# Preactivated deformable convolution: three bands of hats ahead, window turns between the pairs, hat rows at a pitch of 8,640 bytes

## The reference

```python
x = x + _L0_conv_ref(_gn(x), Wa, ba, Wb, bb, Wg, bg, Wo, bo)   # a, b, gate, product, output
x = x + _L1_conv_ref(_gn(x), w_off, b_off, w_def)              # deformable 3x3 convolution
```

```python
x = relu(x)
offset = conv3x3(x, w_off) + b_off                 # 18 channels: dy, dx for each of 9 taps
py = base_y + off[:, :, 0]; px = base_x + off[:, :, 1]
samp = bilinear_gather(x, py, px)                  # zero outside the image
out = einsum('bckhw,ock->bohw', samp, w_def)
```

## Time and profile before

| | |
|---|---|
| median of three executions | 1771.32 us |
| the profiled execution | 1764.54 us |
| its span, first to last instruction | 1762.7 us |
| mean granted TensorE clock | 0.976 of full speed |
| TensorE (PE) busy | 1562.9 us, 89% |
| VectorE (DVE) busy | 1103.9 us, 63% |
| ScalarE (ACT) busy | 974.2 us, 55% |
| GpSimd (POOL) busy | 939.1 us, 53% |
| moved by DMA | 337.09 MB, mean 191 GB/s |

### The profile page before, as it was taken

The page is one execution under the profiler, slowest core; times in us unless marked ns, Lnnn a source line. Parts: engine busy times, 40 slices in busy tenths (PEclk is TensorE's granted clock), DMA queues, the critical chain, the costliest instruction groups (busy, mean ns, idle before and its releaser), DMA issues.

```text
span 1762.7 us, 28712 instructions
## 1 busy us (share of the span) xinstructions
PE 1562.9 (89%) x10451; PEld 1150.9 (65%) x10452; DVE 1103.9 (63%) x1908; ACT 974.2 (55%) x1474; POOL 939.1 (53%) x734
## 2 busy tenths in 40 slices
PE   5999999538889999999999989899999899999998
PEld 3787777416666666666666656666666666666665
DVE  6888888625666666555565655656666565565653
ACT  3555555335556655565655655555655566655552
POOL 2555556326555665565565555555565555556552
PEclk9999999759999999999999999999999999999999
DMA  4343343235656666666666666666666666666652
GB/s 141 101 122 114 112 123 106 97 136 209 205 202 208 223 224 217 218 226 224 216 223 219 222 212 209 218 210 226 220 239 209 227 218 218 219 213 220 207 208 89
DMA packets 146137, 337.09 MB, mean 191 GB/s; under 512 B 10697, under 2 KB 77796, under 8 KB 146020
## 3 DMA queue, kind: packets, MB, share of 16 engines
q1 hardware_dynamic: 131620, 309.58, 51.6%
q10 hardware_dynamic: 14400, 25.96, 4.2%
HBM read 273.54 MB, written 61.95 MB: 190 GB/s over the span
## 4 chain that ended last, share of the span: by engine, by line
DMA 46%; POOL 16%; PE 15%; issue 13%; DVE 5%; SPq 3%; ACT 2%; POOLq 0%; ACTq 0%; DVEq 0%
DMA hx_all<-hat_x 41%; POOL weights L1550 10%; PE bank L745 5%; PE pair L717 4%; POOL x_bo L1504 4%; SPq L532 3%; DMA hat_x<-hats 3%; PE pair L790 2%; DVE hats L1280 1%; ACT dist L948 1%; DMA raw<-x_pad 1%; POOL rstd L1478 1%; PE bank L763 1%; POOL xT_lo L1491 1%; PE pair L728 1%
## 5 line engine op out<-in xcount | busy, mean ns | idle before, releaser
L1550 POOL TENSOR_TENSOR weights<-hy_all,hx_all 120x512 f32<-120x512 f32 x576 | 761.7, 1350 | 636.4 <-DMA hx_all<-hat_x 630.1
L745 PE MATMUL bank<-weights,zT 120*128 120x216 f32 (+1 forms) x2816 | 610.5, 347 | 29.2 <-POOL weights L1550 25.2
L745 PEld LDWEIGHTS bank<-weights,zT 120*128 120x128 f32 x2816 | 508.4, 192 | 109.5 <-POOL weights L1550 44.2
L1293 DVE SCALAR_TENSOR_TENSOR samples_lo<-bank,samples_hi 128x432 f16<-128x432 f32 (+1 forms) x704 | 401.8, 590 | 260.5 <-ACT samples_hi L963 253.1
L963 ACT ACTIVATE samples_hi<-bank 128x432 f16<-128x432 f32 (+1 forms) x704 | 364.5, 519 | 296.6 <-PE bank L745 284.3
L717 PE MATMUL pair<-samples_hi,w_hi 128*128 128x512 f16 x576 | 220.2, 382 | 0.9 <-DVE y L1328 0.9
L921 ACT ACTIVATE z<-raw,norm_band 128x690 f32<-128x690 f32 (+2 forms) x128 | 204.9, 1603 | 26.1 <-DMA raw<-x_pad 24.1
L717 PE MATMUL pair<-samples_lo,w_hi 128*128 128x512 f16 x576 | 219.1, 380 | 0.0
L717 PE MATMUL pair<-samples_hi,w_lo 128*128 128x512 f16 x576 | 219.0, 380 | 0.0
L763 PE MATMUL bank<-ident,z 128*120 128x128 f32 x640 | 106.8, 281 | 80.6 <-DVE zT L1314 80.6
L973 ACT COPY zT<-pair 120x512 f32<-120x512 f32 x192 | 112.1, 584 | 75.2 <-DVE hats L1280 43.4
(11 more groups left out here) (144 smaller groups left out, 2079.7 us busy)
## 6 DMA issues: line engine op xcount, KB each, us to landing
hy_all<-hat_y SPq DMA_DIRECT2D x192, 600.0 KB
hx_all<-hat_x SPq DMA_DIRECT2D x192, 600.0 KB
raw<-x_pad SPq DMA_DIRECT2D x68, 276.0 KB, 15.6
x_pad<-hy_all SPq DMA_DIRECT2D x64, 276.0 KB, 3.7
weights<-in_x SPq DMA_DIRECT2D x64, 256.0 KB, 2.9
out<-y SPq DMA_DIRECT2D x64, 256.0 KB, 15.6
hat_x<-hats ACTq DMA_DIRECT2D x64, 216.0 KB
hat_y<-hats ACTq DMA_DIRECT2D x64, 180.0 KB
```

Source lines behind the costliest of these rows:

```text
L745: mm = nc.tensor.matmul(sampled_pair(b)[:, :, at:at + BR * cols], zT[0:WPIX, u, w, :], weights[0:WPIX, u, :, w * WC * BR:(w * WC + cols) * ...
L1293: nc.vector.scalar_tensor_tensor(out=samples_lo[:, u, :, c0:c1], in0=sampled_pair(b)[:, :, 0:c1 - c0], scalar=PIXEL_SCALE, in1=samples_hi[ ...
L1550: nc.gpsimd.tensor_tensor(weights[0:WPIX, u, tap, :], hy_all[0:WPIX, k, :], hx_all[0:WPIX, k, :], ALU.mult).then_inc(weights_ready, 1)
```

## The change

Four things change.

1. The hats are made and stored three bands ahead and not two (`O`, `Q`, `H` at 3), and their place in DRAM has three slots and three semaphores (`AHEAD`). `z` stays at three bands ahead, and moves from behind the middle of the iteration to its start, in front of the offsets.
2. The windows are turned two bands ahead and not one (`T` at 2). The six groups stand apart between the pairs, each behind the pairs of the current band that still read the windows it overwrites (`pairs_until`).
3. `split_offsets`, `make_hats` and the farthest distance get places of their own in the order (`P`, `G`, `R`), as has the cast of `z` (`h`). The prologues go; the loop starts three iterations earlier with the steps that have a band.
4. In DRAM a hat row of 6,144 bytes starts every 8,640 bytes (`PITCH`) and not every 6,144.

Size and number of all transfers and of all instructions stay the same.

```diff
@@ -28,6 +28,7 @@
 PADC = (WINDOWS - 1) * WC + SRC_C
 BLOCKS = -(-PADR // BR)
 RING = 9
+AHEAD = 3
 BW = BR * WW
 PAIRS = WINDOWS // 2
 TGROUPS = -(-WINDOWS // 4)
@@ -54,6 +55,7 @@
 SUM_ROWS = CONST_AT + 3
 TROWS = 3
 CHUNK = TROWS * BW
+PITCH = 2 * 1024 + 112
 IN_OFF = 16 * 3
 IN_SELECT, SELECT_STEPS = 16 * 9, 8
 BAND_STEPS, ROW_STEPS = 12, 2 + 4 * TAPS
@@ -105,8 +107,8 @@
         x1_pad = nc.dram_tensor("x1_pad", [IMGS, CH, BLOCKS * BR, PADC], F32, kind="Internal").ap()
-        hat_rows = [nc.dram_tensor("hat_y", [2, TROWS, SRC_R, CHUNK], F32, kind="Internal").ap(),
-                    nc.dram_tensor("hat_x", [2, TROWS, SRC_C, CHUNK], F32, kind="Internal").ap()]
+        hat_rows = [nc.dram_tensor("hat_y", [AHEAD, TROWS * SRC_R, PITCH], F32, kind="Internal").ap(),
+                    nc.dram_tensor("hat_x", [AHEAD, TROWS * SRC_C, PITCH], F32, kind="Internal").ap()]
         pairs = [ctx.enter_context(nc.psum_tensor(f"pair{i}", [P, 2, 512], F32)) for i in range(2)]
@@ -287,7 +289,7 @@
         located = sem("located")
         dist_ready = sem("dist_ready")
         reached = sem("reached")
-        hat_out = [sem(f"hat_out{s}") for s in range(2)]
+        hat_out = [sem(f"hat_out{s}") for s in range(AHEAD)]
         hat_in = [sem(f"hat_in{g}") for g in range(TROWS)]
         hats_ready = sem("hats_ready")
         hats_cleared = sem("hats_cleared")
@@ -372,6 +374,10 @@
             na = (TGROUPS + 1) // 2
             return n * na + a, n * (TGROUPS - na) + v
+        def pairs_until(n, g):
+            return PAIRS * n + min(2 * g + 2, PAIRS)
         def pair_before(n, p):
             return PAIRS * n + p - 3 if p > 2 else PAIRS * (n - 1) + (9, 10, 8)[p]
@@ -385,12 +391,12 @@
         ORDER = [(step[0], int(step[1:])) for step in (
-            "k0 O0 s0 s1 s2 Q0 k1 T0 k2 s3 H0 T1 T2 k3 s4 T3 s5 T4 k4 T5 c0 s6 c1 z0 k5 s7 "
-            "c2 c3 z1 k6 s8 c4 c5 k7 s9 c6 k8 s10 c7 c8").split()]
-        def landed(n, u, step):
-            return step * (n // 2 + 1)
+            "z0 s0 c0 s1 k0 T0 z1 s2 c1 k1 s3 T1 h0 k2 c2 s4 s5 O0 T2 k3 c3 P0 s6 k4 c4 s7 T3 Q0 "
+            "c5 k5 G0 s8 c6 k6 H0 s9 R0 T4 k7 c7 s10 T5 k8 c8").split()]
+        def hats_landed(n):
+            return hat_out[n % AHEAD], 32 * (n // AHEAD + 1)
         def first_block(n):
@@ -405,21 +411,15 @@
             return raw_in[block % RING], 16 * (block // RING + 1)
-        def bands(eng, stages, prologue):
-            prologue()
-            def band(n, u):
+        def bands(eng, stages):
+            ahead = {"c": -1, "s": 0, "k": 1, "T": 2, "z": 3, "h": 3, "O": 3, "P": 3, "Q": 3,
+                     "G": 3, "H": 3, "R": 3}
+            for n in range(-AHEAD, BANDS + 1):
                 for kind, j in ORDER:
-                    ahead = {"c": -1, "s": 0, "k": 1, "T": 1, "O": 2, "Q": 2, "H": 2, "z": 3}[kind]
-                    if not 0 <= n + ahead < BANDS:
-                        continue
-                    if kind in stages:
-                        stages[kind](n + ahead, (u + ahead) % 2, j)
-            for n in range(BANDS + 1):
-                band(n, n % 2)
+                    m = n + ahead[kind]
+                    if kind in stages and 0 <= m < BANDS:
+                        stages[kind](m, m % 2, j)
         block = ctx.enter_context(nc.Block())
@@ -520,14 +520,17 @@
                 sp.dma_start(out_v[bass.ds(n // BPI, 1), :, bass.ds(n % BPI * BW, BW)]
                              .rearrange("b c q -> (b c) q"), y[:, s, :]).then_inc(y_out[s], 16)
-            def spread_hats(n, s):
-                sp.wait_ge(hat_out[s], landed(n, s, 32))
+            def spread_hats(n):
+                sp.wait_ge(*hats_landed(n))
                 for g in range(TROWS):
                     wait(sp, weights_ready, TAPS * (n - 1) + TROWS * (g + 1))
-                    rows = [hat_rows[0][s, g].rearrange("(o r) c -> o r c", o=1),
-                            hat_rows[1][s, g, g:g + NEAR_C].rearrange("(r o) c -> r o c", o=1)]
+                    y_at, x_at = g * SRC_R, g * SRC_C + g
+                    rows = [hat_rows[0][n % AHEAD, y_at:y_at + SRC_R, 0:CHUNK]
+                            .rearrange("(o r) c -> o r c", o=1),
+                            hat_rows[1][n % AHEAD, x_at:x_at + NEAR_C, 0:CHUNK]
+                            .rearrange("(r o) c -> r o c", o=1)]
                     for dst, src in zip((hy_flat, hx_flat), rows):
                         sp.dma_start(dst[g * SRC_R:(g + NEAR_C) * SRC_R,
                                          g * CHUNK:(g + 1) * CHUNK],
@@ -537,8 +540,8 @@
             for block in range(RING):
                 load_block(block)
             sp.wait_ge(hats_cleared, 2)
-            spread_hats(0, 0)
-            spread_hats(1, 1)
+            spread_hats(0)
+            spread_hats(1)
             for n in range(BANDS + 2):
                 if n >= 2:
@@ -547,7 +550,7 @@
                     if last_band(block) == n - 2:
                         load_block(block + RING)
                 if n + 2 < BANDS:
-                    spread_hats(n + 2, n % 2)
+                    spread_hats(n + 2)
             for s in range(2):
                 sp.wait_ge(y_out[s], 16 * BANDS // 2)
@@ -798,18 +801,9 @@
                 wait(pe, dist_ready, n)
                 convolve_offset_parts().then_inc(off_done, 1)
-            def prologue():
...
-            bands(pe, {"c": conv, "Q": locate, "s": sample, "T": turn_windows,
-                       "O": offsets}, prologue)
+            pe.wait_ge(select_set, SELECT_STEPS)
+            pe.wait_ge(scaling, W_STEPS)
+            bands(pe, {"c": conv, "Q": locate, "s": sample, "T": turn_windows, "O": offsets})
@@ -924,9 +918,10 @@
                     ACT.Relu,
                     bias=norm_band[:, 1].rearrange("p b n -> p (b n)")[:, n:n + 1],
                     scale=norm_band[:, 0].rearrange("p b n -> p (b n)")[:, n:n + 1])
-                if half == 0:
-                    return
-                done.then_inc(z_ready, 1)
+                if half == 1:
+                    done.then_inc(z_ready, 1)
+            def cast_z(n, u, _):
                 act.wait_ge(z_ready, n + 1)
                 wait(act, off_done, n)
                 nc.scalar.activation(z_hi[:], z[:, u, MARGIN - 1:MARGIN + 1 + WW,
@@ -951,8 +946,9 @@
                 wait(act, hats_ready, n + 1)
                 for axis, rows in enumerate((Y_ROWS, X_ROWS)):
-                    act.dma_start(hat_rows[axis][u].rearrange("g r (k c) -> (g r k) c", k=TROWS),
-                                  hats[0:rows, axis, :]).then_inc(hat_out[u], 16)
+                    act.dma_start(hat_rows[axis][n % AHEAD, :, 0:CHUNK]
+                                  .rearrange("q (k c) -> q k c", k=TROWS),
+                                  hats[0:rows, axis, :]).then_inc(hat_out[n % AHEAD], 16)
             def copy_samples(n, u, p):
                 b = p % 3
@@ -967,33 +963,16 @@
                 if g % 2:
                     return
                 wait(act, z_turned, TGROUPS * n + g + 1)
-                if g == 0:
-                    wait(act, sampled, PAIRS * (n - 1))
+                wait(act, sampled, pairs_until(n - 2, g))
                 c = min(4, WINDOWS - 4 * g)
                 nc.scalar.copy(zT[0:WPIX, u, 4 * g:4 * g + c, :].rearrange("p w c -> p (w c)"),
                                bank[B_ZT[0]][0:WPIX, 0:c * P]).then_inc(zT_a, 1)
-            def prologue():
...
-            bands(act, {"Q": distances, "H": store_hats, "s": copy_samples, "T": copy_windows, "z": make_z,
-                        "O": evict_offsets}, prologue)
+            act.wait_ge(select_set, SELECT_STEPS)
+            act.wait_ge(scaling, W_STEPS)
+            act.wait_ge(final, FINAL_STEPS)
+            bands(act, {"Q": distances, "H": store_hats, "s": copy_samples, "T": copy_windows,
+                        "z": make_z, "h": cast_z, "O": evict_offsets})
         @block.vector
@@ -1275,10 +1254,13 @@
             def make_hats(n, u, _):
                 dve.wait_ge(dist_ready, n + 1)
-                if not isinstance(n, int) or n > 0:
-                    dve.wait_ge(hat_out[1 - u], landed(n - 1, 1 - u, 32))
+                if n > 0:
+                    dve.wait_ge(*hats_landed(n - 1))
                 nc.vector.tensor_scalar(hats[:], dist[:], -1.0, 0.0, ALU.add,
                                         ALU.min).then_inc(hats_ready, 1)
+            def reach_of(n, u, _):
+                dve.wait_ge(dist_ready, n + 1)
                 nc.vector.tensor_reduce(farthest[RAW_AT:CONST_AT, bass.ds(n, 1)],
                                         dist[RAW_AT:CONST_AT, 0, :], AX.X,
                                         ALU.max).then_inc(reached, 1)
@@ -1308,8 +1290,7 @@
                 if g % 2 == 0:
                     return
                 dve.wait_ge(z_turned, TGROUPS * n + g + 1)
-                if g == 1:
-                    wait(dve, sampled, PAIRS * (n - 1))
```

(13 more changed lines are left out.)

37 lines of the change are left out of this document (removed).

## The result

The changed kernel takes 1781.41 us (median of 12 executions, 1773.14 to 1788.34); the kernel before, beside it, 1766.43 (1758.33 to 1778.25). The ratio is 1.0078, interval 1.0052 to 1.0104: slower by 0.8%, in the band that the prediction called within 1%. The forecast was 1728, with a range to 1766. The profiled execution took 1786.2 us, its span 1784.3, at a clock of 0.978.

The account below looks back on a forecast made before the run. Ten DMA engines loading the hats were taken as the bound, TensorE close behind. 385 + 63 x 20.4 + 25 us, then 26.8 to the end, gave span 1722 and forecast 1728 us, range 1690 to 1766.

Parts of the forecast that it names:

- within 1%: Whole kernel: outcome too close to the median to tell from no change, given 0.19, mostly from waits only changing their place.
- What bounds the kernel: Hats' loads: GpSimd waits for them and TensorE for GpSimd; ten DMA engines carry 20.0 us of the 21.3 us band.
- the hole behind the stores: Hats' load stream: SP's first load, held by the stores, leaves a gap; 1.3 us a band would go.
- The ten engines are the bound: DMA loads of 100 partitions by ten broadcasts use ten of 16 engines, busy 20.0 us of 21.3 a band.
- the next limit of 18.9 us: TensorE's pairs, taps, offsets, distances and windows: 18.9 us of work a band, close behind the DMA engines.
- Stores a band earlier: Hats' stores: landing before SP wants them, they remove the loads' hole, so the engines' period falls from 21.3 to 20.0 us.
- TensorE's waits: TensorE in the new order: 1.5 us a band at the first tap and the offsets, making the period 20.4 us.
- The pitch: Hat rows in DRAM: moves row starts, neither bytes nor packets; taken as nothing, bounds 1 us a band either way.
- The rival that saw the pitch as slower: Hats' loads lengthened by rows off a boundary: 10% longer gives period 21.7 and 1806 us; chance 0.12.
- `z` in front: ScalarE's first step at the change of images: loses 17 us once, then some 2 us in each of four iterations, 25 together.
- The start: Before the first band: first load at 360.7 us, 23.9 us on to the weights, first pair at 385.
- The sum: Whole kernel: 385 + 63 x 20.4 + 25, then 26.8 to the end: span 1722, forecast 1728 us.

## Why the prediction was wrong, point by point

- **What bounds the kernel.** That GpSimd waited for the loads, and the hole behind the stores, were read rightly. "The ten engines are the bound" was half of it: without half of the loads the kernel before is slower, 22.0 us a band, since GpSimd then runs over VectorE's halves of the offsets. The limit behind the loads moves with what GpSimd does, and the next limit of 18.9 us, TensorE's need alone, counted none of it. The need itself came out near: 21.2 less 2.0 of waits is 19.2 in the changed kernel.
- **Stores a band earlier: right in effect.** The chain lost DMA, though no run has this part alone. SP's wait for the stores is 3.6 us a band where under 1 was forecast, but it is covered. The load queue's share fell from 57.3% to 56.0%, where a rise was forecast, since the period didn't shrink.
- **TensorE's waits.** 1.5 us a band were forecast, and 20.4 for the period. Measured are 2.0 in the changed kernel (1.05 for `y`, 0.99 for `z_lo`) and 21.2; without the pitch 1.3, and mostly 20.2 to 20.7, 20.5 on average. For the new order alone the term was right. That 1728 stands so near to the 1731.27 of the kernel without the pitch is luck in part: the spans, 1722 and 1728.9, differ by 7 us, and the median of three from which 1728 was scaled lies 5 us above that of twelve.
- **The pitch: the step that failed.** "It moves the starts of the rows that the ten engines read, and neither bytes nor packets. Nothing in the trace prices it. I take nothing". That counted the transfers. It did not count the instruction that issues them, whose shape had changed in the order of the changed kernel, and which stands in front of a pair's copy. The two issues took 1.62 us instead of 0.71, and the pitch as a whole cost 50 us, 0.8 a band: 0.56 of them through `y`, where the runs show the issue as the cause, and 0.2 through `z_lo`, where they leave it open. The rival that saw the pitch as slower had the sign, but put it on the loads: those got some 2% longer, off the path.
- **`z` in front.** 25 us were forecast, 33 measured. The first iteration lost 9.5 and not 17 (30.7 us, about 38 was forecast, with 10.8 us of waiting for `raw` instead of over 12). The next four lost about 6 each (4.8 to 6.4) and not 2. Their blocks did land 4.7 us after their issue (median from 1039 to 1147 us), close to the 5.0 of the forecast; but `y`, the issue of the load and `z` stand around that, so each still waits, 7.0 us at the second. The 2 us of the forecast left little for these.
- **The start.** The first band's weights are complete at 391.45 us, and 385 was forecast from 395.9. In the changed kernel:

```profile
364.62 0.85 SPq L535 DMA_DIRECT2D hy_all<-hat_y  x1
...
387.11 4.34 POOL L1515 TENSOR_TENSOR weights<-hy_all,hx_all 120x512 f32<-120x512 f32 x3 [2.18 <-DMA hx_all<-hat_x]
```

The first load came 3.9 us later than forecast, of which about 3 us are the first part of this execution, which ended later. From there to the weights it took 26.8 us, 2.9 more than the 23.9 that were to stay.

- **The sum.** 0.76 us a band is 48, the change of images 8 and the start 6.5: 62 on the forecast span of 1722 give 1784, and 1784.3 was the span. The measured 1781 lies above the range to 1766, whose upper end came from TensorE's waits and the stores, and whose allowance for the pitch was sized on the loads alone.

## What to carry to other kernels

A layout change in DRAM alters the instruction that issues the transfer as well as the transfer: look at the shape of each DMA in the order of both kernels, and at what stands behind it on that engine. Before an engine is called the bound, take work away from it; here that made the kernel slower, since the engine that it had held back then ran over another's critical instructions. And where a step is moved to the front of an iteration, look at the one place where its input is late: here the price was paid in each of five iterations.
